# Routed experts of a two-layer transformer kernel: from all tokens through all experts to sorted tiles of tokens, with the turns written out as straight code

## The reference, cut to what matters

```python
logits = jax.nn.relu(xf @ Wr1 + br1) @ Wr2 + br2
gates = jax.nn.softmax(logits, axis=-1)
tg, ti = jax.lax.top_k(gates, K)            # K = 2
tg = jax.nn.softmax(tg / K, axis=-1)
out = jax.nn.silu(xf @ Ws1 + bs1) @ Ws2 + bs2
for e in range(E):                          # E = 8, hidden size I = 512
    h = jax.nn.silu(xf @ We1[e] + be1[e]) @ We2[e] + be2[e]
    w = jnp.sum(tg * (ti == e), axis=-1)
    out = out + w[:, None] * h
```

## Time and profile before

| | |
|---|---|
| runs | 1618.66, 1623.88, 1624.66 us |
| profiled execution, its own time | 1616.24 us |
| its span | 1614.5 us |
| granted TensorE clock, mean | 0.966 of full |
| PE matmul busy | 91% |
| DVE busy | 69% |
| ACT busy | 51% |
| POOL busy | 6% |

### The profile page before, as it was taken

One profiled execution on the slowest core, in us unless ns is written; L12 is line 12 of the kernel. 1 busy time (PEld: TensorE's weight loads), 2 busy tenths in 40 slices (PEclk: granted clock), 3 DMA queues, 4 the chain that ended last, 5 costly groups with the idle time before them and its releaser, 6 DMA issues.

```text
span 1614.5 us, 23856 instructions
## 1 busy us (share of the span) xinstructions
PE 1465.2 (91%) x8221; PEld 663.5 (41%) x8253; DVE 1112.0 (69%) x2019; ACT 822.1 (51%) x1007; POOL 102.7 (6%) x138
## 2 busy tenths in 40 slices
PE   2689999999989999889998999999998999997997
PEld 1124552245523554245532455234542355423561
DVE  8976884778756787567956688477875678653660
ACT  1164238742576426754277423874257642684336
POOL 5001000110000100010001100001000100001000
PEclk7689999999999999999999999999999999997999
DMA  4404300241002400034000420024100240000300
GB/s 114 160 16 140 87 2 9 68 129 47 2 16 87 128 22 2 16 113 123 2 2 30 148 73 1 9 72 130 42 2 16 91 130 16 2 9 28 90 2 7
DMA packets 93994, 87.90 MB, mean 54 GB/s; under 512 B 12890, under 2 KB 93091, under 8 KB 93619
## 3 DMA queue, kind: packets, MB, share of 16 engines
q1 hardware_dynamic: 92258, 83.59, 17.1%
q0 software_dynamic: 672, 2.16, 0.5%
q10 hardware_dynamic: 944, 0.54, 0.1%
HBM read 45.87 MB, written 39.85 MB: 53 GB/s over the span
## 4 chain that ended last, share of the span: by engine, by line
PE 53%; DVE 21%; issue 14%; DVEq 5%; ACT 4%; POOL 2%; SPq 0%; DMA 0%; ACTq 0%; POOLq 0%
PE ring L970 15%; PE sums L1141 14%; DVE nm L743 8%; PE mx L1091 8%; PE sums L1083 7%; PE mx L1039 5%; ACT ex L563 3%; DVEq L825 2%; PE ring L976 2%; DVE macc L831 2%; PE ring L1039 2%; DVE xn L671 1%; PE ring L965 1%; POOL parts L470 1%; DVE h_sb L719 1%
## 5 line engine op out<-in xcount | busy, mean ns | idle before, releaser
L563 ACT ACTIVATE ex<-mx 128x1024 f32<-128x1024 f32 x512 | 497.2, 1027 | 162.2 <-PE mx L1091 161.7
L743 DVE TENSOR_REDUCE nm<-mx 128x2 f32<-128x1024 f32 x428 | 501.2, 1216 | 85.6 <-PE mx L1039 81.4
L605 ACT ACTIVATE ex<-ring,b_sb 128x512 f32<-128x512 f32 x288 | 197.1, 687 | 421.5 <-PE ring L970 421.4
L1141 PEld LDWEIGHTS sums<-w_sb,ex 128*128 128x128 f32 x2304 | 283.5, 191 | 94.8 <-issue 89.9
L1141 PE MATMUL sums<-w_sb,ex 128*128 128x128 f32 x2304 | 319.3, 283 | 0.4
L970 PE MATMUL ring<-xnT,w_sb 128*128 128x512 f32 x576 | 297.6, 602 | 2.0 <-ACT ex L605 2.0
L1091 PE MATMUL mx<-qs,ks 74*128 74x512 bf16 (+1 forms) x992 | 274.8, 385 | 15.7 <-ACT ex L563 6.6
L1083 PE MATMUL sums<-ex,vs 128*18 128x512 f32 x2048 | 269.0, 600 | 14.4 <-issue 13.8
L1091 PEld LDWEIGHTS mx<-qs,ks 128*128 128x128 bf16 (+1 forms) x1024 | 75.9, 98 | 261.8 <-ACT ex L563 235.4
L1039 PE MATMUL mx<-ks,qs 64*128 64x512 bf16 x856 | 149.4, 396 | 36.0 <-DVE nm L743 34.8
L747 DVE TENSOR_REDUCE nm<-ring 128x1 f32<-128x512 f32 x168 | 108.2, 686 | 72.3 <-PE ring L1039 71.9
(11 more groups left out here) (135 smaller groups left out, 1017.2 us busy)
## 6 DMA issues: line engine op xcount, KB each, us to landing
scratch<-parts SPq DMA_DIRECT2D x64, 384.0 KB, 4.0
ks<-scratch SPq DMA_DIRECT2D x256, 64.0 KB, 2.2
qs<-scratch SPq DMA_DIRECT2D x256, 64.0 KB, 2.2
scratch<-parts SPq DMA_DIRECT2D x32, 256.0 KB, 4.1
w_sb<-w SPq DMA_DIRECT2D x2, 2304.0 KB
rest<-parts SPq DMA_DIRECT2D x32, 128.0 KB, 3.2
x_sb<-x SPq DMA_DIRECT2D x8, 256.0 KB, 2.8
out<-macc POOLq DMA_DIRECT2D x8, 256.0 KB, 3.8
```

Source lines behind the costliest of these rows:

```text
L563: act.activation(ex[:, ex_buffer(l, k), 2 * i:2 * i + 2, :], mx[bank][:, :, :], ACT.Exp, scale=SCALE).then_inc(mx_free[bank], 1)
L605: act.activation(ex[:, e % 2, c, :], bank[:, :], ACT.Silu, bias=b1_sb[:, e * EC + c:e * EC + c + 1]).then_inc(free, 1)
L743: dve.tensor_reduce(nm[l][:, t, h:h + 2], mx[bank][:, :, :], AX.X, ALU.max, negate=True).then_inc(mx_free[bank], 1)
L1141: last = pe.matmul(acc[bank][:, t * P:(t + 1) * P], ex[:, e % 2, c, t * P:(t + 1) * P], w2_sb[:, e, c, :], start=c == 0, stop=c == EC - 1)
```

## The change

The shared expert stays as it was, with its weights in SBUF. The routed experts are computed on sorted tokens. DVE builds from the router's two choices a 0/1 matrix, PE counts by products with constant matrices how many tokens precede each one at its expert (`ranks`), and DVE derives each token's two places in a list in which every expert starts at a multiple of 128 (`places`). The list has NTILE = 15 tiles of 128 rows. POOL scatters the tokens by 8 indirect DMAs of 128 rows of 512 bytes into `x_sorted` in HBM, loads that back in 4 groups, fetches the weights of each tile's expert by an indirect DMA (128 rows of 4,112 bytes, 526 KB) into one of NW = 4 buffers, stores the tiles' outputs to `o_sorted` in HBM, and gathers them by 8 more indirect DMAs. DVE adds them with their weights in slot 13 of layer 1. PE transposes the sorted tokens, and for each tile computes 4 products for the hidden part (128 columns each) and 4 for the output. The 48 pairs of maxima of the stage are laid out anew: 12 of layer 0 in six steps beside the shared expert, the 32 of layer 1 over tiles 0 to 12, and 4 of layer 0 beside tiles 13 and 14. `max_rows(1)` stands at tile 13.

The loops over turns become Python loops on all five engines: the turns are straight code. At the start, POOL makes some constants and clears `x_sorted`, and the resident expert weights that SP loads shrink from 4.6 MB to 0.5 MB. The diff, cut:

```diff
+NX = NE - 1
 EC = FE // P
+NTILE = (2 * T + NX * (P - 1)) // P
+TG = 4
+NTG = (NTILE + TG - 1) // TG
+NW = 4
...
+M1_TILE = NTILE - 2
+COMBINE_SLOT = SLOTS - 3
...
-M1_BY_EXPERT = [0, 0, 0, 4, 8, 8, 6, 6, 0]
+M0_STEPS = [2, 2, 2, 2, 2, 2]
+M0_TILES = [2, 2]
+ROUND = 1.5 * 2.0 ** 30
...
+def maxima_of_tile(i):
+    if i < M1_TILE:
+        return [(1, pair) for pair in range(NPAIR * i // M1_TILE, NPAIR * (i + 1) // M1_TILE)]
+    first = M0_IN_PROJECTION + sum(M0_STEPS) + sum(M0_TILES[:i - M1_TILE])
+    return [(0, first + n) for n in range(M0_TILES[i - M1_TILE])]
...
-            with sp.Fori(0, B - 1) as it:
+            for it in range(B - 1):
                 turn(it, "turn")
...
+            def fetch_weights(it, i):
+                n = it * NTILE + i
+                if n >= NW:
+                    pool.wait_ge(tile_done, n - NW + 1)
+                pool.indirect_dma_start(wx_sb[n % NW][:, :], None, wx, bass.IndirectOffsetOnAxis(ap=wx_row[:, i:i + 1], axis=0)).then_inc(wx_in[n % NW], 16)
+            def store_tiles(part, it, g):
+                bank, before = accs.at(part, it, ("O", g))
+                pool.wait_ge(acc_free[bank], before + 2)
+                tiles = tiles_of_group(g)
+                rows = o_sorted[tiles.start * P:tiles.stop * P, :].rearrange("(i p) c -> p i c", p=P)
+                pool.dma_start(rows, xs[:, tiles.start:tiles.stop, :]).then_inc(os_out, 16)
+            def experts(part, it):
+                pool.wait_ge(slots_ready, it + 1)
+                for n in range(2):
+                    for t in range(NT):
+                        pool.indirect_dma_start(x_sorted, bass.IndirectOffsetOnAxis(ap=slot[:, n, t:t + 1], axis=0), xn[1][:, t, :], None).then_inc(xs_out, 16)
+                fetch_weights(it, 0)
+                fetch_weights(it, 1)
+                pool.wait_ge(xs_out, (it + 1) * 16 * 2 * NT)
+                for g in range(NTG):
+                    tiles = tiles_of_group(g)
+                    rows = x_sorted[tiles.start * P:tiles.stop * P, :].rearrange("(i p) c -> p i c", p=P)
+                    pool.dma_start(xs[:, tiles.start:tiles.stop, :], rows).then_inc(xs_in[g], 16)
+                for i in range(2, NTILE):
+                    if i >= 2 * TG and i % TG == 0:
+                        store_tiles(part, it, i // TG - 2)
+                    fetch_weights(it, i)
+                store_tiles(part, it, NTG - 2)
+                store_tiles(part, it, NTG - 1)
+                pool.wait_ge(os_out, (it + 1) * 16 * NTG)
+                for n in range(2):
+                    for t in range(NT):
+                        pool.indirect_dma_start(moe[:, n, t, :], None, o_sorted, bass.IndirectOffsetOnAxis(ap=slot[:, n, t:t + 1], axis=0)).then_inc(moe_in, 16)
...
                 residual1(it)
                 third_part(1, it)
+                experts("turn", it)
                 store_out("turn", it)
...
+            def sorted_tokens(part, it, g):
+                copy_out(part, it, ("X", g), xsT[:, g % 2, 0:len(tiles_of_group(g)) * P], width=len(tiles_of_group(g)) * P)
+            def tile_silu(part, it, i):
+                n = it * NTILE + i
+                bank, free = from_ring(part, it, ("Ht", i))
+                if n >= TG:
+                    act.wait_ge(tile_done, n - TG + 1)
+                for c in range(EC):
+                    last = act.activation(ex[:, 1, c, i % TG * P:i % TG * P + P], bank[:, c * P:(c + 1) * P], ACT.Silu,
+                                          bias=wx_sb[n % NW][:, FE + c:FE + c + 1])
+                last.then_inc(free, 1)
+            def tiles_out(part, it, g):
+                tiles = tiles_of_group(g)
+                act.wait_ge(tile_done, it * NTILE + tiles.stop)
+                bank = accs.at(part, it, ("O", g))[0]
+                act.copy(xs[:, tiles.start:tiles.stop, :].rearrange("p i c -> p (i c)"), acc[bank][:, 0:len(tiles) * P]).then_inc(acc_free[bank], 1)
...
+                act.wait_ge(pv_done, slots_before(1, it))
+                for c in range(EC):
+                    bank, free = from_ring(part, it, ("H", c))
+                    act.activation(ex[:, 0, c, :], bank[:, :], ACT.Silu, bias=b1_sb[:, c:c + 1]).then_inc(free, 1)
+                    if c == 1:
                         act.wait_ge(lgd_ready, it + 1)
                         act.activation(le[:, :, :], le[:, :, :], ACT.Exp).then_inc(le_ready, 1)
...
+                act.wait_ge(gd_ready, it + 1)
+                act.activation(e2[:, :], e2[:, :], ACT.Tanh, scale=0.25).then_inc(e2_ready, 1)
+                copy_out(part, it, "wT", w9T[:, :], rows=NE)
+                sorted_tokens(part, it, 0)
+                for i in range(NTILE):
+                    tile_silu(part, it, i)
+                    if i % TG == TG - 2 and i // TG + 1 < NTG:
+                        sorted_tokens(part, it, i // TG + 1)
+                    if i % TG == 1 and i >= TG:
+                        tiles_out(part, it, i // TG - 1)
+                exponentials(1, part, it, it, 0)
+                tiles_out(part, it, NTG - 1)
+                for k in range(1, SLOTS):
                     exponentials(1, part, it, it, k)
...
+                dve.drain()
+                dve.tensor_tensor(choices[:, :, :], chosen[:, 0, :, :], chosen[:, 1, :, :], ALU.add).then_inc(choice_ready, 1)
+            def places(part, it):
+                bank, free = from_ring(part, it, "rank")
+                n_before, n_all = bank[:, 0:NT * NX].rearrange("p (t e) -> p t e", e=NX), bank[:, NT * NX:(NT + 1) * NX]
+                dve.tensor_scalar(padded[:, :], n_all, (P - 1) / 2.0, ROUND, ALU.add, ALU.add)
+                dve.drain()
...
+                dve.tensor_tensor(place[:, :, :], n_before, start[:, :].unsqueeze(1).broadcast_to([P, NT, NX]), ALU.add).then_inc(free, 1)
+                dve.tensor_tensor(starts_by[:, :, :], start[:, 1:NX].unsqueeze(1).broadcast_to([P, NTILE, NX - 1]),
...
+                dve.tensor_copy(wx_row[:, :], tile_row[:, :])
+                dve.drain()
+                dve.tensor_copy(slot[:, :, :], slot_f[:, :, :]).then_inc(slots_ready, 1)
...
+            def add_experts(part, it):
+                dve.wait_ge(moe_in, (it + 1) * 16 * 2 * NT)
+                for n in range(2):
+                    dve.drain()
+                    for t in range(NT):
+                        dve.scalar_tensor_tensor(macc[:, t, :], moe[:, n, t, :], tg[:, t, n:n + 1], macc[:, t, :], ALU.mult, ALU.add)
+                dve.drain()
...
+                choose(part, it)
+                step_maxima(0)
+                places(part, it)
+                gate_difference(part, it)
+                step_maxima(1)
+                router_weights(part, it)
+                step_maxima(2)
+                add_shared(part, it)
+                step_maxima(3)
+                step_maxima(4)
+                step_maxima(5)
+                add_biases(part, it)
+                for i in range(NTILE):
+                    if i == M1_TILE:
+                        max_rows(1, part, it, it)
+                    for l, pair in maxima_of_tile(i):
+                        if l == 1 or not last:
+                            maxima(l, part, it, pair)
...
                         sums_out(1, part, it, 0)
+                    if k == COMBINE_SLOT:
+                        add_experts(part, it)
...
+            def ranks(part, it):
+                pe.wait_ge(choice_ready, it + 1)
+                bank, full = to_ring(part, it, "rank")
+                pe.matmul(bank[:, 0:NX], earlier[:, :], choices[:, 0, :], start=True, stop=True)
...
+                last.then_inc(full, 1)
...
+            def sorted_tokens(part, it, g):
+                pe.wait_ge(xs_in[g], (it + 1) * 16)
+                bank, full = to_ring(part, it, ("X", g))
+                for i in tiles_of_group(g):
+                    last = pe.transpose(bank[:, i % TG * P:(i % TG + 1) * P], xs[:, i, :], ident[:, :])
+                last.then_inc(full, 1)
+            def tile_hidden(part, it, i):
+                n = it * NTILE + i
+                pe.wait_ge(wx_in[n % NW], (n // NW + 1) * 16)
+                if i % TG == 0:
+                    read_out(pe, part, it, ("X", i // TG))
+                bank, full = to_ring(part, it, ("Ht", i))
+                for c in range(EC):
+                    last = pe.matmul(bank[:, c * P:(c + 1) * P], wx_sb[n % NW][:, c * P:(c + 1) * P],
+                                     xsT[:, i // TG % 2, i % TG * P:i % TG * P + P], start=True, stop=True)
+                last.then_inc(full, 1)
+            def tile_out(part, it, i):
+                n = it * NTILE + i
+                if i % TG == 0:
+                    to_sums(part, it, ("O", i // TG))
+                read_out(pe, part, it, ("Ht", i))
+                bank = accs.at(part, it, ("O", i // TG))[0]
+                for c in range(EC):
```

(43 more changed lines are left out.)

242 lines of the change are left out of this document (129 added, 113 removed).

## The result

The changed kernel took 1635.2 us in the median of 12 runs, the kernel before beside it 1622.0: a ratio of 1.0077, 95% interval [1.0052, 1.0101], so 0.8% slower. Beside later runs on another chip it was 1.0070 [1.0038, 1.0101]. The forecast was 1566 us, faster.

The account below looks back on a forecast made before the run. PE was taken to bound the stage (busy 84.0 of 85.9 us), DVE next. Gains of 4.5 + 0.9 + 2.3 = 7.7 us in seven turns and 4.3 in the last, together 58.2, gave 1566 us; range 1525 to 1690.

Parts of the forecast that it names:

- Free while c stays under 2.4 us.: Layer-1 slots: the gathers end near 828 us, before slot 13 at about 836, and so cost no time.
- c: POOL's cost of one indirect DMA, taken as 1.2 us, between 0.8 and 3.8.
- landing of the load back, issue of 0.8 and 2.8 us: Ahead of tile 0: sorted rows loaded back by 755.0 us, so that tile 0 starts at 756.5.
- fit inside: Ahead of tile 0: two weight fetches issued during the last scatter's landing of 3.8 us add no time.
- first rival: Eight scatters ahead of tile 0: POOL's indirect DMAs cost more, at c = 3.0 us 1681 us in all; chance 0.23.
- Tiles: Tiles 0 to 12: DVE sets the pace at 3.03 us a tile, 40.5 us, plus 2.0 us for the clock.
- Rows of maxima: Ahead of the first slot: the slots could start about 7.4 us after the transposes of the maxima.
- Straight code: At the loop's edge: seven edges go, each saving 2.3 us of PE idle time, bounds 0 and 2.5.
- The faster case: Whole kernel: c = 0.8 and no clock loss give 12.2 us a turn, 9.8 in the last, 1529 us; chance 0.15.
- PE's share: Whole kernel: PE's busy time falls by some 220 us and its share to about 80%.
- one recovery of the clock: Steps ahead of the tiles: PE coming out of a gap at lower clock was charged once, 2.0 us.
- Where the tile starts past 759 I am wrong: Start of the tiles: forecast at 756.5 us; the prediction called itself wrong if later than 759.

Follow-up runs that it names:

- a_again: The changed kernel unaltered, run once more on one chip beside two other kernels: 1632.9 us, 1.0070 of the kernel before.
- a_gather_pairs: The changed kernel with POOL waiting for the landing after every second of the eight gathers: 1592.2 us, 0.9819 of the kernel before.
- a_three_again: a_scatter_three unaltered, run once more on the same chip as a_again: 1588.0 us, 0.9775 of the kernel before.
- a_scatter_three: The changed kernel with gathers in waited-for pairs and never more than three scatters under way: 1590.7 us, 0.9792 of the kernel before.
- a_scatter_fours: The changed kernel with gathers in waited-for pairs and scatters in two groups of four, each waited for: 1612.8 us, 0.9941 of the kernel before.
- a_rows_first: The changed kernel with the weight fetches of tiles 0 and 1 issued behind the first load of sorted rows: 1631.7 us, 1.0059 of the kernel before.
- a_one_ahead: a_scatter_three with the weights of tile 0 fetched ahead of the scatters: 1582.2 us, 0.9765 of the kernel before.
- a_two_ahead: a_one_ahead with the weights of tiles 0 and 1 both fetched ahead of the scatters: 1602.7 us, 0.9884 of the kernel before.
- a_one_again: a_one_ahead unaltered, run once more beside another kernel on one chip: 1583.6 us, 0.9753 of the kernel before.
- a_maxima_first: a_one_again with 4 of the 32 pairs of layer-1 maxima taken ahead of the first tile: 1592.2 us, 0.9816 of the kernel before.
- a_direct: The changed kernel with each scatter and gather replaced by a direct DMA of the same size, tokens not sorted: 1551.9 us, 0.9568 of the kernel before.
- straight form: The kernel before with only its loop over turns written out as straight code: 1602.8 us, 0.9878 of the kernel before.
- three useless series: The straightened kernel before with otherwise useless DMA series from POOL, another kind each turn, in three versions: 1606.2, 1610.9 and 1601.8 us.

## Why the prediction was wrong, step by step

Three stretches of a turn, as means over the turns of each execution, from PE's timelines: first slot to the next turn's ranks; ranks to first tile; first tile to first slot.

```
                 slot to ranks   ranks to tile   tile to slot
changed kernel       115.3           26.3            50.3
a_again              115.4           26.5            49.9
a_gather_pairs       109.5           26.7            49.7
a_three_again        110.2           26.8            50.1
a_scatter_three      109.8           26.7            50.1
a_scatter_fours      109.5           29.3            49.9
a_rows_first         114.4           24.4            52.7
a_one_ahead          109.5           25.5            49.8
a_two_ahead          109.7           27.7            49.9
a_one_again          109.9           25.9            50.0
a_maxima_first       110.2           29.5            46.5
a_direct             110.0           21.0            51.1
```

**The step that failed is the gathers' "Free while c stays under 2.4 us."** c was under that (and under the 2.2 us that the sum's own terms give), the last gather was issued by 828.8 and slot 13 waited for nothing; the additions of 2.35 us at 848.56 lay in idle time. But I asked only who waits for the gathers, and not what issuing them does to engines that have nothing to do with them. Unbroken, they cost 5.8 us a turn (115.3 against 109.5): seven times, and 2.4 to 6.9 us in the last turn (from its first slot to the end 51.7 against 49.3, and 55.7 against 48.8), make 43 to 48 us. The pairs gave back 43 between the medians, and 45 on one chip (a_again and a_three_again). Set Exp against Exp, the two kernels show where. In the fourth turn ACT's sixth pair of Exps starts at 823.86 and at 803.98 in a_gather_pairs, 19.88 apart; the seventh is 2.9 us later, the ninth (835.08 against 810.81) 4.4 us later, and from there the distance stays. Between the two PE ran at 0.57 of its clock, with 1.91 us for a group of sums that takes 1.05 otherwise; in a_gather_pairs the clock is 1.00 there. Over the seven turns the distance settles at 3.1 to 5.0 us, once at 9.4, as a mean 5.1 of the 5.8. So the cost is the stall and the half clock right behind it.

**The second is the landing of the load back, issue of 0.8 and 2.8 us.** From its issue to the first transposes 7.3 us went by in the fourth turn, 6.0 to 7.3 in all of them, since the load stood behind two fetches of 526 KB in POOL's queue (the page's 7.5 is the median of all 24 full loads). The first tile started at 761.0, forecast 756.5; the stage had started 1.1 us later, so 3.4 us are the stage's own. I had let the two fetches "fit inside" the scatters' landing by POOL's time, and not by the queue's bytes. The page "DMA: Bandwidth & Descriptors" of the Trainium skill, section "Anatomy of one DMA — SWDGE (gpsimd) path", gives a fixed 2.0 us and the bytes for one DMA, an estimate of 2.6 us here; a DMA with 1.05 MB ahead of it is not one DMA, and the measured 6.0 to 7.3 us decide. But the term could not simply be won: a_rows_first took it back and paid in weights.

The whole account, from the two profiled executions (spans 1614.5 and 1635.1, 20.6 us apart), cut at the first product of the shared expert and at the first slot:

```
                                      before   forecast   measured   missed by
stage, mean of seven turns             85.9      81.4       84.0     7 x 2.6
stage, last turn                       83.8      80.4       86.9         6.5
first slot to the next turn's stage   104.5     101.3      107.6     7 x 6.3
last first slot to the end             46.6      45.7       55.7        10.0
```

That makes 79 us, the forecast gain of 58 and the loss of 20.6 together. The slots and the end, where the gathers are, have 54 of them and the stage 25. With the gathers in pairs the last two rows are 101.7 and 48.8 us: the stretch from slot to stage came out nearly as forecast.

**The hold at the scatters**, for all its length, costs nothing that can be seen: 26.7 us from ranks to tile with holds (a_gather_pairs) and without any (a_scatter_three). It is covered by the sorted rows' way. (The kernels ran on different chips; in the kernel before, with nothing to cover it, a series of scatters cost 7 to 9 us.)

**What was right.** *c:* 0.96 to 0.98 us of POOL and 1.26 from start to start, forecast 1.2; eight scatters took 10.2 us, and the load back was issued at 751.88, forecast 751.4. The first rival is out. The rule of the page "GPSIMD Engine Reference" of the Trainium skill (section "7. Performance pitfalls for Q7 kernels") would make it 10.9 us by my estimate; these DMAs do not pay that. *Tiles:* 43.4 us from the first to the transposes of the maxima, forecast 42.5. *Rows of maxima:* 7.3 us, forecast 7.4. *Straight code:* 18 us in seven edges, 2.6 each, forecast 2.3. *The faster case:* its 9.8 us in the last turn should be 8.8 by its own terms, 1 us of no weight. *PE's share:* 82%, forecast about 80; but its busy time fell by 119 us and not by 220. I charged one recovery of the clock, and the windows show 0.66 over 21.6 us ahead of the first tile, 0.93 in the tiles and 0.80 in the slots. *Where the tile starts past 759 I am wrong*, the prediction said; it started at 761.0, or 759.9 from the same start of the stage. The range, 1525 to 1690, held the time, for reasons that none of its rivals named.

## What to carry to other kernels

Before you move work from a busy engine to an idle one, price what its use does to the others: here unbroken series of eight indirect DMAs beside the slots cost some 44 us over the kernel, and a wait after every second of them, on an engine with time to spare, gave it back. What is issued behind bulk data on one queue lands behind it, so count the queue's bytes and not the issuing engine's time. And run variants that are to be compared in one session on one chip: two of mine looked cured, and three useless series harmless, only because of where they ran.

The best version found, 1582 to 1584 us, beats the kernel before by 2.4%, and by the ratios its straight form (0.9878, in another session) by 1.2%.
